# Exponentials over three PSUM banks instead of two in a decoder's self-attention

## What is computed

```
q, k, v = quat_linear(x, W, b)              # q and k then divided by a quaternion norm
p = exp(scale * k q^T)                      # for each batch and head, 1024 keys x 1024 queries
o = (v^T p) / sum over keys of p            # then the output projection
x = layernorm(x + o)
```

## Time and profile before

| | us |
|---|---|
| runs before | 793.13, 793.65, 1197.72 |
| median | 793.65 |
| profiled execution | 796.66 |
| its span | 794.9 |
| the attention's exponentials, first and last start | 58.4 and 305.3 |

### The profile page before, as it was taken

The page is one execution under the profiler, slowest core; times in us unless marked ns, Lnnn a source line. Parts: engine busy times, 40 slices in busy tenths (PEclk is TensorE's granted clock), DMA queues, the critical chain, the costliest instruction groups (busy, mean ns, idle before and its releaser), DMA issues.

```text
span 794.9 us, 10723 instructions
## 1 busy us (share of the span) xinstructions
PE 710.1 (89%) x3774; PEld 386.9 (49%) x3774; DVE 519.3 (65%) x1216; ACT 554.1 (70%) x973; POOL 196.9 (25%) x230
## 2 busy tenths in 40 slices
PE   4999999899999999999999999779898999991596
PEld 2552222112222225888888886544455644440485
DVE  3695645932422224587657557979976687988886
ACT  3659999899999996564042345587787533898991
POOL 1662142200110000102552242455543100000022
PEclk9999999999999999999999999989999999996699
DMA  6312212321256160303326000010100000000002
GB/s 200 126 27 42 39 27 67 53 67 27 36 131 193 28 179 1 106 2 106 109 104 212 1 1 0 1 56 25 40 1 1 1 1 0 0 1 0 0 28 79
DMA packets 57373, 42.12 MB, mean 53 GB/s; under 512 B 36866, under 2 KB 54120, under 8 KB 57192
## 3 DMA queue, kind: packets, MB, share of 16 engines
q1 hardware_dynamic: 57176, 41.31, 18.4%
q10 hardware_dynamic: 144, 0.13, 0.1%
HBM read 28.59 MB, written 4.46 MB: 42 GB/s over the span
## 4 chain that ended last, share of the span: by engine, by line
PE 56%; ACT 22%; DVE 16%; issue 3%; DMA 1%; SPq 1%; POOL 1%; POOLq 0%; DVEq 0%; ACTq 0%
ACT arena L638 12%; PE banks L1640 8%; PE banks L2189 7%; PE banks L1938 7%; PE banks L1954 6%; PE banks L1626 4%; PE banks L1610 3%; PE banks L1968 2%; DVE arena L1470 2%; DVE arena L1030 2%; PE banks L1800 2%; PE banks L2072 2%; PE banks L2027 1%; ACT arena L846 1%; ACT arena L857 1%
## 5 line engine op out<-in xcount | busy, mean ns | idle before, releaser
L638 ACT ACTIVATE arena<-banks 128x1024 f32<-128x1024 f32 x256 | 239.8, 1045 | 8.5 <-PE banks L1640 6.1
L1640 PE MATMUL banks<-arena 128*32 128x512 f32 x1024 | 137.5, 609 | 4.2 <-DVE arena L1107 4.0
L1626 PE MATMUL banks<-arena 64*128 64x512 f16 x512 | 86.6, 385 | 9.2 <-ACT arena L638 6.0
L2189 PE MATMUL banks<-arena 128*128 128x512 f32 x192 | 83.1, 593 | 1.1 <-DVE arena L1486 0.9
L758 ACT ACTIVATE arena<-banks,arena 128x77 f32<-128x77 f32 x256 | 59.2, 368 | 21.0 <-DVE arena L1386 21.0
L392 POOL TENSOR_SCALAR arena<-arena 128x2 f32<-128x2 f32 (+1 forms) x38 | 11.9, 313 | 250.2 <-DVE arena L1033 250.2
L1626 PEld LDWEIGHTS banks<-arena 64*128 64x128 f16 x512 | 20.9, 93 | 108.6 <-ACT arena L638 98.3
L2197 PE MATMUL banks<-arena 128*128 128x256 f32 x192 | 43.6, 391 | 26.8 <-ACT arena L867 26.8
L716 ACT ACTIVATE arena<-banks,arena 128x256 f32<-128x256 f32 x64 | 26.9, 471 | 53.0 <-PE banks L1938 53.0
L2189 PEld LDWEIGHTS banks<-arena 128*128 128x128 f32 x192 | 36.2, 190 | 47.4 <-issue 43.4
L1954 PE MATMUL banks<-arena 128*128 128x256 f32 x256 | 56.6, 380 | 0.0
(11 more groups left out here) (254 smaller groups left out, 1265.6 us busy)
## 6 DMA issues: line engine op xcount, KB each, us to landing
arena<-in_L_ffn_w SPq DMA_DIRECT2D x16, 1024.0 KB, 7.4
w_kept<-arena SPq DMA_DIRECT2D x3, 768.0 KB, 3.6
arena<-w_kept SPq DMA_DIRECT2D x3, 768.0 KB, 4.8
arena<-in_x SPq DMA_DIRECT2D x4, 512.0 KB, 8.8
out_x<-arena SPq DMA_DIRECT2D x3, 512.0 KB, 2.9
arena<-in_L_ffn_b SPq DMA_DIRECT2D x1, 1024.0 KB, 8.7
arena<-in_L_ffn_w_gate SPq DMA_DIRECT2D x1, 768.0 KB, 7.8
arena<-in_L_ffn_w_up SPq DMA_DIRECT2D x1, 768.0 KB, 9.5
```

What stands on the lines that cost most here:

```text
L638: act.activation(PT[kt % 2][:, half], PS[:, 2 * (n % 3):2 * (n % 3) + 2, :], ACT.Exp, scale=DH ** -0.5 / QK_UP ** 2).then_inc(sem("exp_don ...
L1626: mm = pe.matmul(bank(2 * (n % 3) + h), KT[u % 2][64 * h:64 * h + 64, P * kt:P * kt + P], QT[u % 2][64 * h:64 * h + 64, 512 * half:512 * h ...
L1640: mm = pe.matmul(PS[32 * j:32 * j + 32, 6, :], VS[w][:, kt, h, :], PT[kt % 2][:, half, h, :], start=(kt == 0), stop=(kt == TB - 1))
L2189: mm = pe.matmul(bank(2 + n % 4), (wgT if n < IC * G4 else wuT)[:, k, P * c:P * c + P], XT[:, k, 512 * g:512 * g + 512], start=(k == 0), s ...
```

## The change

The 512 slots of all units are numbered through. A set is now three slots, whatever step or unit they belong to: 171 sets, the last with two slots. Two groups of three banks take turns (banks 0 to 2, 3 to 5), so set n waits for exponential n - 2. One exponential covers the set. PT becomes four tiles of three slots, the fourth in words 8072 to 10120, where raw weights of the quaternion layers lay before the attention. Before the values of a step, all sets up to the second after the one with the step's last slot are issued. On VectorE, `late_qn` for tile 14 moves behind unit 5's copy to OSB.

```diff
+SLOTS = 4 * TB * UN
+SETS = -(-SLOTS // 3)
...
-        PT = [att(2, 2, 512) for _ in range(2)]
+        PT = [att(3, 512) for _ in range(3)]
+        PT.append(Bump(8072, 10120)(3, 512))
...
                 if u >= 2:
-                    sp.wait_ge(sem("qk_done"), 2 * TB * (u - 1))
+                    sp.wait_ge(sem("qk_done"), -(-4 * TB * (u - 1) // 3))
...
-            def exps(u, kt):
-                for half in range(2):
-                    n = 2 * (TB * u + kt) + half
-                    act.wait_ge(sem("qk_done"), n + 1)
-                    if half == 0 and TB * u + kt >= 2:
-                        act.wait_ge(sem("pv_done"), TB * u + kt - 1)
-                    act.activation(PT[kt % 2][:, half], PS[:, 2 * (n % 3):2 * (n % 3) + 2, :], ACT.Exp,
-                                   scale=DH ** -0.5 / QK_UP ** 2).then_inc(sem("exp_done"), 1)
-
-            for u in range(UN):
-                for kt in range(TB):
-                    exps(u, kt)
+            def exps(n):
+                act.wait_ge(sem("qk_done"), n + 1)
+                if 3 * n >= 10:
+                    act.wait_ge(sem("pv_done"), (3 * n - 10) // 4 + 1)
+                w = min(3, SLOTS - 3 * n)
+                act.activation(PT[n % 4][:, 0:w], PS[:, 3 * (n % 2):3 * (n % 2) + w, :], ACT.Exp,
+                               scale=DH ** -0.5 / QK_UP ** 2).then_inc(sem("exp_done"), 1)
+
+            for n in range(SETS):
+                exps(n)
...
                 if u in (HT - TB, HT - TB + 1):
-                    for t in range(HT, T - 1) if u == HT - TB else (T - 1,):
-                        late_qn(t)
+                    late_qn(HT if u == HT - TB else T - 1)
...
                 dve.tensor_copy(OSB[:, u], bank(6)).then_inc(sem("o_evac"), 1)
+                if u == HT - TB:
+                    late_qn(T - 2)
...
             def scores(n):
 
-                u, kt, half = n // (2 * TB), n // 2 % TB, n % 2
-                if n % (2 * TB) == 0:
-                    pe.wait_ge(sem("q_turned"), 16 * u + 16)
-                    pe.wait_ge(sem("k_turned"), 16 * u + 16)
-                if n >= 3:
-                    pe.wait_ge(sem("exp_done"), n - 2)
-                for h in range(2):
-                    mm = pe.matmul(bank(2 * (n % 3) + h), KT[u % 2][64 * h:64 * h + 64, P * kt:P * kt + P],
+                if n >= 2:
+                    pe.wait_ge(sem("exp_done"), n - 1)
+                for s in range(3 * n, min(3 * n + 3, SLOTS)):
+                    u, kt, half, h = s // (4 * TB), s // 4 % TB, s // 2 % 2, s % 2
+                    if s % (4 * TB) == 0:
+                        pe.wait_ge(sem("q_turned"), 16 * u + 16)
+                        pe.wait_ge(sem("k_turned"), 16 * u + 16)
+                    mm = pe.matmul(bank(3 * (n % 2) + s % 3), KT[u % 2][64 * h:64 * h + 64, P * kt:P * kt + P],
                                    QT[u % 2][64 * h:64 * h + 64, 512 * half:512 * half + 512], start=True, stop=True)
                 mm.then_inc(sem("qk_done"), 1)
 
             def values(u, kt):
                 w = u % 2
-                pe.wait_ge(sem("exp_done"), 2 * (TB * u + kt) + 2)
+                first = 4 * (TB * u + kt)
+                pe.wait_ge(sem("exp_done"), (first + 3) // 3 + 1)
...
-                        j = 2 * h + half
-                        mm = pe.matmul(PS[32 * j:32 * j + 32, 6, :], VS[w][:, kt, h, :], PT[kt % 2][:, half, h, :],
+                        j, s = 2 * h + half, first + 2 * half + h
+                        mm = pe.matmul(PS[32 * j:32 * j + 32, 6, :], VS[w][:, kt, h, :], PT[s // 3 % 4][:, s % 3],
                                        start=(kt == 0), stop=(kt == TB - 1))
...
+            def scored(step):
+                return min((4 * step + 3) // 3 + 3, SETS)
+
             def attn_unit(u):
                 for kt in range(TB):
-                    for n in range(2 * (TB * u + kt) + 3, 2 * (TB * u + kt) + 5):
-                        if n < 2 * TB * UN:
-                            scores(n)
+                    for n in range(max(2, scored(TB * u + kt - 1)), scored(TB * u + kt)):
+                        scores(n)
...
-            for n in range(3):
+            for n in range(2):
                 scores(n)
```

## The result

The changed kernel takes 806.26 us in the profiled execution; its runs are 805.78, 806.26, 809.55 and 1810.75 us (the median of all four is 807.9), those of the kernel before 793.13, 793.65, 794.29 and 1197.72. The two runs above 1100 us are left out of the comparison. The ratio is 1.0144, 95% interval 1.0107 to 1.0182, or +11.4 us. I had forecast 800.6 and a range of 787 to 808: the direction and the range held, and the size was a little more than half of what came.

The account below looks back on a forecast made before the run. TensorE was taken to bound the 49 steps with side work, ScalarE the 79 plain ones. Terms summed to +6.9 us: 803.6 from the profiled 796.66, or 800.6 against the median 793.65; range 787 to 808.

Parts of the forecast that it names:

- Exponentials: ScalarE in plain steps: wider exponentials, one every 1.344 us, save 0.042 us a step over 79 steps, -3.3 us.
- Scores on TensorE and the slack: Attention steps: single score matmuls cost TensorE +7.4 us in 49 steps; less slack in plain steps costs +1.7.
- high end: TensorE's scores: each single matmul costs a full 0.226 us, since matmuls on one half follow each other; low end nothing.
- Two sets in turn and the boundaries: Attention: only one exponential covers the next scores, +1.0 us; waits for VectorE's copy at unit boundaries pass on, +2.5.
- The deeper store: 12 slots of exponentials against 8 loosen ScalarE's waits for values; costed at nothing, as TensorE bounds those steps.
- The norm: VectorE in unit 5: one norm behind the copy ends TensorE's 1.57 us stall and the half-clock stretch, -2.6 us.
- rival C: Moved norm delays unit 7's query staging and transposes, first scores 1.7 us late; 803 to 808 us; chance 0.07.
- The start: Start of the attention: the first exponential waits for three slots, +0.2 us.
- Clock 1.00 throughout: Sign that the forecast is right: TensorE's granted clock stays full, with no stretch at 0.50.
- Rival B: TensorE's pauses in groups and at unit boundaries bring half-clock stretches, up to 1.7 us each, 826 us; chance 0.04.
- Rival A: Attention: ScalarE stays the bound and the single matmul hides; 787 us, or 784 to 794; chance 0.24.

Follow-up runs that it names:

- kernel with more scores: The kernel before, with every third set's last score matmul done twice, 85 matmuls more; ratio 1.0118.
- sets of three alone: The changed kernel with late_qn of tile 14 put back ahead of unit 5's copy; ratio 1.0131.
- staged kernel: The changed kernel with late_qn of tile 14 in unit 6 behind its staging of queries, in place of ahead of it; ratio 1.0089.

## Why the prediction fell short, step by step

- **Exponentials, -3.3.** The cost is right: 1.343 us a set. How much of it reaches the stage no run separates. By the Trainium skill (ScalarE: Activation LUTs, What ACT_TABLE_LOAD costs), which leaves 93 ns of each fixed when they run back to back, a set would take 1.373 us, an estimate; this trace, with 1.343, does not agree.
- **Scores on TensorE and the slack, +9.1.** Borne out in the main. The kernel with more scores has it alone: +8.5 us, in which unit 6 shrank by 2.0 (17.48 to 15.52) and a half-clock stretch came, some 1.3 to 1.6 us by the other kernels; without these two, +8.9 to +9.2. A single costs 0.226 us, as in the high end that I took, but for the 13 pairs of singles that ran side by side.
- **Two sets in turn and the boundaries, +3.5.** Together with the -3.3 they make +0.2; sets of three against more scores measure +0.8, with the deeper store and the 2.9 us less of scores in it. The sum comes out near; whether it does so because each part is right, the runs do not show. They do not divide it between turn and boundary either.
- **The deeper store, 0.** It is open what it gives in the changed kernel. In the kernel before it is worth 5.2 us of the stage, so "these steps are TensorE's and stay so" was wrong as a reason: there the short waits for values were not free.
- **The norm, -2.6.** The step failed, though the sum hides it. Unit 6 did fall, by 2.35 us in sets of three alone, with the norm where it was: slower units gave VectorE the time, and TensorE waited 0.62 us for the copy and not 1.57. The move itself cost 0.7 us against that kernel and 1.2 against staging first. I had made the sum with unit 5's old timing, on a stage that the other terms made longer. This was rival C, with 0.07: its chain was worked out at 10.2 us against 10.7, and came to 12.2 (from 158.28 to 170.52) against 10.6, since the staging copies ran beside POOL and took 1.59 us, and the last transpose landed 4.0 us after its issue and not 3.2.
- **The start, +0.2.** The wait for the third slot came as priced: from the first score matmul to the first exponential 57.34 to 57.97, 0.63 us against 58.01 to 58.43, 0.42. It lies ahead of the stage as measured here. Two things behind it I had not counted. "Clock 1.00 throughout" failed: a stretch at 1.2 GHz stood in unit 0 of the profiled execution, +1.6 us. Rival B had named such stretches, but at the groups and boundaries, where none came; its cause here is open. And TensorE's two pauses behind the first scores grew from 0.68 and 0.52 us to 1.31 and 0.74; that is most likely in the 1.6 us by which unit 0 is longer even without the stretch (18.59 against 16.96).

The sum can be checked on the staged kernel, which has neither the low clock nor the late transposes: 249.5 + 6.7 (6.9 less the 0.2 ahead of the stage) = 256.2 us, and it measured 256.8. The changed kernel has both: 256.2 + 1.6 + 1.2 = 259.0, and 259.6 were measured. The rest of the 11.4 us is the difference between one profile and the runs. That the sum lands so near is in part luck: two terms in it, the store at nothing and the norm at -2.6, had wrong reasons, and errors of the others may cancel. The signs of rivals B (a stretch at 0.50) and C (unit 7's scores waiting for a transpose) were both seen, in a time of 806.26 us, at the edge of the forecast's 796 to 806.

Rival A, ScalarE as the bound, is out: it would need ScalarE's idle time to stay near 8.5 us, and it is 21.2.

## What to carry to other kernels

Before widening an instruction to save its fixed cost, count what the width does to the engine that feeds it: 85 saved instructions took 5 us of ScalarE's own time here, and the odd tile that mostly had no partner cost TensorE 16 to 19 us, of which some 9 were on the path. Where side work makes steps uneven, one more buffer can be worth more than wider pieces: a third tile for the exponentials won 5.2 us of the stage at no instruction. A stall that is read from one trace is priced for that trace's timing; if other terms of the same change move the unit around it, work it out again with them.

## What the hardware showed that I had not expected

- The same program, run again, had its half-clock stretch in another place and twice as long (57.4 to 64.2 us in place of 62.0 to 65.4), while every unit behind it had the same length within 0.02 us. Differences of 1 to 2 us between kernels of this stage are read unit by unit, not from the totals.
- Four staging copies on VectorE took 1.59 us in place of 0.62 where POOL ran its low halves beside them.
- Two singles of different halves run side by side when the second set need not wait: six score matmuls in 0.82 us, where two sets of three take 0.60 each by themselves.
